# Mamba-and-experts kernel, second layer: decay loads and time steps placed earlier, and five products with C on VectorE in the last batch

## The chip, the core and the metric

The kernel runs on one core of one Trainium2 chip. The metric is the device time of one execution in microseconds. Five engines matter here: TensorE (PE in the profile, with PEld for its weight loads), VectorE (DVE), ScalarE (ACT), GpSimd (POOL) and SyncE (SP), which in this kernel issues nearly all DMAs. Every engine works through its own list of instructions in order, and the lists meet at semaphores.

## The reference

The model has two layers on 8 sequences ("batches") of 512 tokens with 128 features. Layer 0 is attention with a low-rank key and value path, plus a gated feed-forward part. Layer 1 adds a Mamba mixer and a mixture of experts to its input. Of layer 1 the change touches the mixer:

```python
h = _rmsnorm(x, norm_w); xz = h @ in_proj_w; u, z = split(xz)
u = silu(causal_depthwise_conv(u, conv_w, conv_b))
xdbl = u @ x_proj_w                      # dt_r (64), B (16), C (16)
dt = softplus(dt_r @ dt_proj_w + dt_proj_b)
def step(hst, inp):                      # over 512 time steps
    dA = exp(dt_t[..., None] * A)        # 256 channels x 16 states
    dBu = dt_t[..., None] * B_t[:, None, :] * u_t[..., None]
    hst = dA * hst + dBu
    y = einsum('bdn,bn->bd', hst, C_t)
y = (y + u * D) * silu(z);  return x + y @ out_proj_w
```

The experts are a shared gated block for every token and, of eight routed ones, the two best per token. Their rows are sorted into tiles of 256 rows, 24 tiles for each half of the batches; each tile is loaded with its expert's weights, computed and stored, and GpSimd later gathers the results back to the tokens.

## The kernel before

Layer 0 ends at about 483 us. From there the second layer goes through the 8 batches. In each, 256 channels times 16 states make 4096 recurrences, which are held as 32 **groups** of 128 partitions by 512 time steps; the loop variable `k` of every engine's `batch` function counts the groups, and each engine has its own `batch` (lines 1595, 1723, 1851, 1955 and 2102) in which the condition on `k` alone sets what is issued at which step. There is no scheduler: the order of the work on an engine is what these conditions write out. Batch `b` is in the loop while the inputs of batch `b + 1` are prepared (`nxt`) and the end of batch `b - 1` is finished (`old`).

One group goes like this. TensorE spreads dt times u over the states into one of two PSUM buffers (`spread_du`, L2029). VectorE multiplies it by B there (`inject`, L1922) and runs the recurrence with `tensor_tensor_scan` (`scan`, L1931) into one of 12 buffers `hs`. The scan's decays are exp(dt A): ScalarE computes them in place three groups ahead (`decay`, L1826) from dt rows that a DMA has repeated over the 16 states. GpSimd multiplies two groups at a time by C (`times_c`, L1681), and TensorE sums over the states, four groups at a time (`gather_y`, L2038). A scan whose buffer `hs` still holds a group that is not summed waits for `gathered`.

**The loads of decays** (`load_decays`, DMA at L1559) move 1 MB each, for four groups; I call the eight of a batch q0 to q7. There are four buffers for them at a time (their names in the profile are `decays`, `slots` and `y_xr`, since two of them live in memory that other data leave free), so the load for one quarter can start when the scans of the quarter four places before are done. SP waits for that (`scanned`) and for the dt rows to be in DRAM (`store_dt`, L1536).

**The time steps.** For batch `b + 1`: TensorE projects (`x_proj`, `dt_proj`), ScalarE and VectorE compute the softplus in parts (`dt_in`, `exp_z`, `one_more`, `log_in`, `softplus_cut` L1901, `softplus_end` L1906), GpSimd adds its parts and multiplies by u (`steps`, L1669 and L1673), SP stores dt to DRAM and then loads q0. In three bf16 parts dt times u goes to `block_in` through 24 small DMAs (`stack`, L1528), after ScalarE (`first_part`, `second_part`) and VectorE (`second_rest` L1911, `third_part` L1916) have split it.

**The experts** come along a table `plan` of due steps: SP loads rows (`load_rows`, L1499) and weights (`load_weights`, L1508) and stores results (`store_tile`, L1514), TensorE turns and multiplies (`turn_tile` L2048, `gate` L2064, `up`, `down`), ScalarE copies (`copy_xg` L1832, `copy_g` L1838, `weigh` L1845), VectorE and GpSimd do half each of the gated product (`half` L1944, `hidden` L1686). `fetch` (L1720) is the indirect DMA on GpSimd that brings results back; 20 of them stand in batch 8.

**The end of a batch** is `gather_y` of the last four groups, `skip` (L1937, adds u times D), `gate_y` (L1693, times silu z), `out_proj` (L2099) and `result` (L1952), then the store of the output (L1586).

## Time and profile before

| | us |
|---|---|
| median of 3 runs | 1230.9 (1224.32 to 1238.44) |
| the profiled execution, its own time | 1228.28 |
| its span, first to last instruction | 1226.5 |
| busy: DVE / PE / POOL / ACT | 938.6 / 871.2 / 701.0 / 505.5 |
| first scans of batches 1 to 8 | 483.1, 595.0, 689.1, 778.8, 870.1, 960.6, 1050.6, 1133.4 |

The profile is one execution. Its share of busy time is a mean over stages: in layer 0 and in layer 1 different engines are the limit, so the time of a batch of the second layer, from its first scan to the next batch's, is the number to read. Idle time stands in brackets behind the instruction that came after it, with what ended it.

### The profile page before, as it was taken

Reading aid. Unit: us, or ns where it says so; the run is one execution under the profiler, and the core shown is the slowest. Engines: PE = TensorE matmul, PEld = TensorE weight load, DVE = VectorE, ACT = ScalarE, POOL = GpSimd, SP = SyncE. Lnnn points to the kernel's source line nnn. Section 1 sums busy time; section 2 is a strip of 40 time slices with the busy share of each in tenths; the row PEclk is TensorE's granted clock in tenths of the full one; section 3 lists DMA queues with packets and bytes.
Section 4 is the critical chain, followed back from the end, with each engine's and each line's share of the span. In section 5 each row is a group of like instructions: output and inputs, shape, how many; then the busy total and the mean of one; then the engine's idle time right before and its main releaser. Section 6 shows DMA issues by size and latency. Waiting matters only on the chain. (4 is left out here: it accounts for less than half of the span.)

```text
span 1226.5 us, 12808 instructions
## 1 busy us (share of the span) xinstructions
PE 871.2 (71%) x3620; PEld 412.1 (34%) x3620; DVE 938.6 (77%) x1280; ACT 505.5 (41%) x840; POOL 701.0 (57%) x427
## 2 busy tenths in 40 slices
PE   3668988888888656676587687688777688664552
PEld 0123333333333323344244344344434344311120
DVE  3467787977977445799469879688979779899973
ACT  0112212123123322473376386385495485663230
POOL 1021122031113561379569877569989879789996
PEclk9568788788897867699689899797999889875575
DMA  4886746666450352767766766767877767646631
GB/s 127 208 180 144 187 140 153 184 171 152 118 142 14 99 155 63 155 145 165 185 196 176 188 207 167 158 215 172 207 217 169 182 207 174 206 141 126 163 86 28
DMA packets 102849, 192.30 MB, mean 157 GB/s; under 512 B 13147, under 2 KB 68124, under 8 KB 90364
## 3 DMA queue, kind: packets, MB, share of 16 engines
q1 hardware_dynamic: 91516, 183.07, 57.2%
q0 software_dynamic: 11264, 8.43, 4.2%
q8 instruction: 29, 0.48, 0.2%
q14 instruction: 40, 0.33, 0.1%
HBM read 146.80 MB, written 32.06 MB: 146 GB/s over the span
## 5 line engine op out<-in xcount | busy, mean ns | idle before, releaser
L1681 POOL TENSOR_TENSOR hs<-hs,c_rep 128x1024 f32<-128x1024 f32 x128 | 332.0, 2604 | 87.7 <-DVE hs L1931 86.9
L1922 DVE TENSOR_TENSOR p_s_du<-p_s_du,b_rep 128x512 f32<-128x512 f32 x256 | 175.4, 685 | 49.5 <-PE p_s_du L2029 46.2
L2029 PE MATMUL p_s_du<-block_in,spread 96*128 96x512 bf16 x256 | 112.9, 442 | 115.5 <-DVE hs L1931 109.0
L1931 DVE TENSOR_TENSOR_SCAN hs<-decays,p_s_du 128x512 f32<-128x512 f32 x132 | 161.1, 1221 | 13.5 <-DVE p_s_du L1922 0.5
L1931 DVE TENSOR_TENSOR_SCAN hs<-slots,p_s_du 128x512 f32<-128x512 f32 x100 | 122.1, 1221 | 19.7 <-ACT slots L1826 9.7
L802 DVE TENSOR_TENSOR value_prod<-p_eb_y_acc,v 128x512 f32<-128x512 f32 x128 | 83.9, 685 | 56.6 <-PE p_eb_y_acc L1109 47.1
L513 POOL TENSOR_TENSOR sc<-ex,ex_part 128x1024 f32<-128x1024 f32 x8 | 17.0, 2129 | 171.6 <-ACT ex_part L619 171.6
L1826 ACT ACTIVATE decays<-decays,a_neg 128x512 f32<-128x512 f32 x132 | 91.7, 718 | 49.4 <-DMA decays<-dt_rows 39.3
L1720 POOL DMA_INDIRECT y_xr<-moe_sums,position x64 | 105.4, 1647 | 10.8 <-issue 8.2
L1686 POOL TENSOR_TENSOR y_hid<-y_hid,g_in 128x512 f32<-128x512 f32 x64 | 99.0, 1548 | 20.3 <-DVE y_hid L1944 19.8
L2029 PEld LDWEIGHTS p_s_du<-block_in,spread 96*128 96x128 bf16 x256 | 26.1, 102 | 249.4 <-DVE hs L1931 179.0
L2038 PE MATMUL p_eb_y_acc<-hs,gather 128*32 128x512 f32 x512 | 84.3, 737 | 18.1 <-POOL hs L1681 18.1
L1826 ACT ACTIVATE slots<-slots,a_neg 128x512 f32<-128x512 f32 x100 | 68.6, 717 | 69.1 <-DMA slots<-dt_rows 69.0
L778 DVE TENSOR_TENSOR score_prod<-qb,p_k_misc 128x2048 f32<-128x2048 f32 x32 | 72.4, 2282 | 12.8 <-issue 7.4
L2064 PE MATMUL p_a_g<-xgt,wm 128*128 128x256 f32 x192 | 56.2, 419 | 25.6 <-ACT sg L1839 16.0
L1838 ACT ACTIVATE g_in<-p_a_g 128x512 f32<-128x512 f32 x64 | 38.1, 595 | 78.6 <-PE p_a_g L2064 46.7
L530 POOL TENSOR_TENSOR root<-var,half 128x8 f32<-128x8 f32 x8 | 13.2, 1648 | 96.3 <-DVE var L851 96.3
L2091 PE MATMUL p_acc_o<-wm,y_hid 128*128 128x128 f32 x384 | 60.9, 310 | 2.9 <-ACT os L1845 1.8
L2091 PEld LDWEIGHTS p_acc_o<-wm,y_hid 128*128 128x128 f32 x384 | 57.7, 223 | 10.2 <-POOL y_hid L1686 7.5
L2001 PE MATMUL p_k_misc<-y_ht,wtap 128*128 128x512 f32 x112 | 58.3, 618 | 0.0
L1073 PE MATMUL p_s_du<-score_prod,sum_d 128*32 128x512 f32 x256 | 46.8, 813 | 13.0 <-DVE score_prod L778 13.0
L2074 PE MATMUL p_a_u<-xgt,wm 128*128 128x256 f32 x192 | 54.5, 410 | 0.0
(193 smaller groups left out, 1751.6 us busy)
## 6 DMA issues: line engine op xcount, KB each, us to landing
decays<-dt_rows SPq DMA_DIRECT2D x33, 1024.0 KB
qb<-rq_rows SPq DMA_DIRECT2D x32, 1024.0 KB, 13.5
slots<-dt_rows SPq DMA_DIRECT2D x25, 1024.0 KB
wm<-in_wmoe SPq DMA_DIRECT2D x48, 384.0 KB
moe_rows<-zeros SPq DMA_DIRECT2D x8, 774.0 KB, 6.0
xg<-moe_rows SPq DMA_DIRECT2D x48, 129.0 KB
stack<-ex_part SPq DMA_DIRECT2D x96, 64.0 KB
block_in<-y_part SPq DMA_DIRECT2D x192, 32.0 KB
```

Source lines behind the costliest of these rows:

```text
L778: nc.vector.tensor_tensor(score_prod[:, i % 2], qb[:, i], p_k[:].unsqueeze(1).to_broadcast([128, 4, T]), ALU.mult)\
L802: nc.vector.tensor_tensor(value_prod[:, n % NP], p_eb[:, n % 2], v[:, b % NV], ALU.mult).then_inc(weighed.sem, 1)
L1681: nc.gpsimd.tensor_tensor(hs[:, n:n + 2], hs[:, n:n + 2], c_rep[p][:].unsqueeze(1).to_broadcast([128, 2, T]), ALU.mult)\
L1686: nc.gpsimd.tensor_tensor(hid[:, v % 2], hid[:, v % 2], g_in[:, v % 2], ALU.mult).then_inc(hid_done.sem, 1)
L1720: nc.gpsimd.indirect_dma_start(xr[:, b - 1, t], None, moe["sums"][grp], bass.IndirectOffsetOnAxis(ap=position[:, grp, kk, TT * i + t:TT * ...
L1826: nc.scalar.activation(decay_of, decay_of, ACT.Exp, scale=a_neg[:, g:g + 1]).then_inc(da_done.sem, 1)
L1922: nc.vector.tensor_tensor(p_du[:, k % 2], p_du[:, k % 2], b_rep[p][:], ALU.mult).then_inc(dbu_done.sem, 1)
L1931: nc.vector.tensor_tensor_scan(hs[:, n % NA], home(8 * (b - 1) + k // 4)[:, bass.ts(j, T)], p_du[:, k % 2], 0.0, ALU.mult, ALU.add).then_i ...
L2001: ins = nc.tensor.matmul(bank(b, U0 + n)[:, :], wtap[:, k, bass.ts(n, 128)], ht[:, b % 2, k:k + T], start=(k == 0), stop=(k == CONV - 1))
L2029: nc.tensor.matmul(p_du[:, k % 2], spread[:, i], block_in[:, (2 * b + s) % NB, j], start=True, stop=True).then_inc(du_full.sem, 1)
L2038: ins = nc.tensor.matmul(p_y[32 * j:32 * j + 32], w["gather"][:, i], hs[:, (GROUPS * (b - 1) + k) % NA], start=(i == 0), stop=(i == 3))
L2091: ins = nc.tensor.matmul(p_o[:, bass.ts(i, 128)], hid[:, v % 2, 256 * f + 128 * i:256 * f + 128 * i + 128], wm[:, j % NR, 2 * FF1 + 128 * ...
```

## The change

It touches the second layer alone, and every product, sum and load of before is still there. What it does:

- SP: the loads q3 to q7 of a batch move from steps 2, 6, 10, 14, 18 to 0, 4, 8, 12, 16; those of q0, q1, q2 of the next batch from 22, 26, 30 to 22, 24, 28. Within a step the decay load now comes first, then weights, then rows. Stores of expert tiles are issued two steps later, `repeat_bc` three later, `store_dt` and the first half of `stack` one sooner.
- The chain of time steps is one step sooner on TensorE and ScalarE, two on VectorE and GpSimd; on GpSimd `steps` and `hidden` now stand ahead of `times_c` in their step. The parts (`first_part` to `third_part`) are one step sooner.
- `gather_y` of the last quarter is one step sooner (2 for 3); `out_proj` and `result` are four steps later in all but the last batch (13 and 15 for 9 and 11).
- In batch 8 the products with C of pairs 3, 6, 9, 12 and 15 are done by VectorE right behind the scan of the pair's second group, in a new function; GpSimd does the other eleven. `gather_y` waits for both counts.

```diff
@@ -1319,6 +1319,7 @@
     QS = 30
     AHEAD = 3
     PAIRS = 5
+    BY_VECTOR = (3, 6, 9, 12, 15)
     SEG = GROUPS // ST
     TAPS = {14: (0, (0,)), 16: (0, (1,)), 17: (0, (2,)), 18: (0, (3,)), 20: (1, (0, 1)), 21: (1, (2,)), 22: (1, (3,))}
     shared, position, tile_expert, slots, second = w["shared"], moe["position"], moe["tile_expert"], moe["slots"], moe["second"]
@@ -1443,7 +1445,7 @@
                     plan.append((dict(rows=begin_at - 8 + 2 * h, weights=begin_at - 6 + 2 * h, turn=begin_at + h, gate=begin_at + 2 + h,
                                       hidden=then + 2 if h else begin_at + 6, up=then if h else begin_at + 4,
                                       half=then + 1 if h else begin_at + 5, down=then + 5 if h else then + 1,
-                                      weigh=then + 6 if h else then + 2, store=then + 8 if h else then + 4),
+                                      weigh=then + 6 if h else then + 2, store=then + 10 if h else then + 6),
                                  b, h, tile, len(plan) + 1))
     tile_unit = {tile: v for _, _, _, tile, v in plan if tile is not None}
 
@@ -1608,20 +1610,20 @@
                     tail(k)
                     if k == 23:
                         load_xr(0)
+                if b == 1 and k in (4, 8, 12, 15, 18):
+                    load_decays(1, {4: 3, 8: 4, 12: 5, 15: 6, 18: 7}[k])
+                if 1 < b <= B and k % 4 == 0 and k < 20:
+                    load_decays(b, (k + 12) // 4)
+                if nxt and k in (22, 24, 28):
+                    load_decays(b + 1, (k - 20) // 4)
+                for _, _, j, _ in due(b, k, "weights"):
+                    if j is not None:
+                        load_weights(j)
                 for _, _, j, _ in due(b, k, "rows"):
                     if j is not None:
                         load_rows(j)
-                for _, _, j, _ in due(b, k, "weights"):
-                    if j is not None:
-                        load_weights(j)
-                if b == 1 and k in (4, 8, 12, 15, 18):
-                    load_decays(1, {4: 3, 8: 4, 12: 5, 15: 6, 18: 7}[k])
-                if 1 < b <= B and k % 4 == 2 and k < 20:
-                    load_decays(b, (k + 10) // 4)
                 if b == 4 and k == 30:
                     load_xr(1)
-                if nxt and k % 4 == 2 and k > 20:
-                    load_decays(b + 1, (k - 22) // 4)
                 for _, _, j, _ in due(b, k, "store"):
                     if j is not None:
                         store_tile(j)
@@ -1633,12 +1635,12 @@
                 if nxt:
                     if k == 10:
                         store_bc(b + 1)
-                    if k == 16:
+                    if k == 19:
                         repeat_bc(b + 1, 1 - p)
-                    if k in (19, 21):
-                        store_dt(b + 1, (k - 19) // 2)
-                    if k in (21, 23, 24):
-                        stack(b + 1, 0, (21, 23, 24).index(k))
+                    if k in (18, 20):
+                        store_dt(b + 1, (k - 18) // 2)
+                    if k in (20, 22, 23):
+                        stack(b + 1, 0, (20, 22, 23).index(k))
                     if k in (25, 26, 27):
                         stack(b + 1, 1, k - 25)
                 if b == 7 and k in (1, 2, 3, 4):
@@ -1729,18 +1731,18 @@
                 turn = GROUPS * (b - 1) + k - 14
                 if 0 <= turn < 4 * GT and turn % 2 == 0:
                     send(*divmod(turn // 2, GT))
-                if old and k == 0:
-                    times_c(b - 1, q, GROUPS // 2 - 1)
-                if new and k and k % 2 == 0:
-                    times_c(b, p, k // 2 - 1)
+                if nxt and k in (16, 18):
+                    steps(b + 1, q, (k - 16) // 2)
                 for _, _, j, v in due(b, k, "hidden"):
                     hidden(v)
+                if old and k == 0 and b <= B:
+                    times_c(b - 1, q, GROUPS // 2 - 1)
+                if new and k and k % 2 == 0 and not (b == B and k // 2 - 1 in BY_VECTOR):
+                    times_c(b, p, k // 2 - 1)
                 if old and k == 5:
                     gate_y(b - 1, q, 1)
                 if new and k == 21:
                     gate_y(b, p, 0)
-                if nxt and k in (18, 20):
-                    steps(b + 1, q, (k - 18) // 2)
                 if (b, k) in bring:
                     fetch(*bring[b, k])
 
@@ -1872,20 +1874,19 @@
                 if k == 5:
                     silu_u(b + 1, q)
                     silu_z(b + 1, q)
-                if k == 9:
+                if k == 8:
                     copy_xd(b + 1)
-                if k in (11, 13):
-                    dt_in(b + 1, (k - 11) // 2)
+                if k in (10, 12):
+                    dt_in(b + 1, (k - 10) // 2)
+                if k == 12:
+                    exp_z(b + 1)
                 if k == 13:
-                    exp_z(b + 1)
-                if k == 14:
                     one_more(b + 1)
-                if k == 15:
                     log_in(b + 1)
-                if k in (20, 23):
-                    first_part(b + 1, (k - 20) // 3)
-                if k in (22, 25):
-                    second_part(b + 1, (k - 22) // 3)
+                if k in (19, 22):
+                    first_part(b + 1, (k - 19) // 3)
+                if k in (21, 24):
+                    second_part(b + 1, (k - 21) // 3)
 
         def main(tail):
             act.wait_ge(before["x1"].sem, before["x1"].at(B))
@@ -1931,6 +1932,12 @@
             nc.vector.tensor_tensor_scan(hs[:, n % NA], home(8 * (b - 1) + k // 4)[:, bass.ts(j, T)], p_du[:, k % 2],
                                          0.0, ALU.mult, ALU.add).then_inc(scanned.sem, 1)
 
+        def times_c(p, i):
+            dve.wait_ge(scanned.sem, scanned.at(B, 2 * i + 2))
+            n = (GROUPS * (B - 1) + 2 * i) % NA
+            nc.vector.tensor_tensor(hs[:, n:n + 2], hs[:, n:n + 2], c_rep[p][:].unsqueeze(1).to_broadcast([128, 2, T]), ALU.mult)\
+                .then_inc(hc_too.sem, 1)
+
         def skip(b, p, s):
             dve.wait_ge(gathered.sem, gathered.at(b, 4 * s + 4))
             dve.wait_ge(y_done.sem, y_done.at(b, s) if s else y_done.at(b - 1))
@@ -1958,26 +1965,28 @@
                 if new:
                     inject(b, p, k)
                     scan(b, k)
+                if b == B and k % 2 and k // 2 in BY_VECTOR:
+                    times_c(p, k // 2)
                 if tail:
                     tail(k)
                 for _, _, j, v in due(b, k, "half"):
                     half(v)
                 if old and k == 4:
                     skip(b - 1, q, 1)
-                if old and k == 11:
+                if old and k == (15 if nxt else 11):
                     result(b - 1)
                 if new and k == 20:
                     skip(b, p, 0)
                 if not nxt:
                     continue
-                if k == 16:
+                if k == 14:
                     softplus_cut(b + 1)
-                if k == 17:
+                if k == 15:
                     softplus_end(b + 1)
-                if k in (21, 24):
-                    second_rest(b + 1, (k - 21) // 3)
-                if k in (22, 26):
-                    third_part(b + 1, (k - 22) // 4)
+                if k in (20, 23):
+                    second_rest(b + 1, (k - 20) // 3)
+                if k in (21, 25):
+                    third_part(b + 1, (k - 21) // 4)
 
         def main(tail):
             schedule(batch, tail)
@@ -2030,7 +2039,12 @@
 
         def gather_y(b, q):
 
-            pe.wait_ge(hc_done.sem, hc_done.at(b, 2 * q + 2))
+            if b == B:
+                of_vector = sum(i < 2 * q + 2 for i in BY_VECTOR)
+                pe.wait_ge(hc_too.sem, hc_too.at(1, of_vector))
+                pe.wait_ge(hc_done.sem, hc_done.at(b, 2 * q + 2 - of_vector))
+            else:
+                pe.wait_ge(hc_done.sem, hc_done.at(b, 2 * q + 2))
             if q % 4 == 0:
                 pe.wait_ge(y1_done.sem, y1_done.at(b, q // 4) if q else y1_done.at(b - 1))
             for k in range(4 * q, 4 * q + 4):
@@ -2118,10 +2132,10 @@
                 for c, m, j, v in due(b, k, "down"):
                     down(v, c, m, j)
                 if nxt:
-                    if k == 8:
+                    if k == 7:
                         x_proj(b + 1, q)
-                    if k in (10, 12):
-                        dt_proj(b + 1, (k - 10) // 2)
+                    if k in (9, 11):
+                        dt_proj(b + 1, (k - 9) // 2)
                 if b + 2 <= B:
                     if k in TAPS:
                         project_u(b + 2, *TAPS[k])
@@ -2130,9 +2144,9 @@
                 if new:
                     if k >= 7 and k % 4 == 3:
                         gather_y(b, (k - 7) // 4)
-                if old and k == 3:
+                if old and k == 2:
                     gather_y(b - 1, GROUPS // 4 - 1)
-                if old and k == 9:
+                if old and k == (13 if nxt else 9):
                     out_proj(b - 1, 1)
                 if new and k == 24:
                     out_proj(b, 0)
```

Two places where the written order shows best. The first is SP's list near the end of batch 5, from the load of batch 6's q0 (its first row) over q1 to q2 (its last row); `slots` and `decays` are the buffers loaded. Before:

```order
411 L1559 DMA decays<-dt_rows 128x1x2048
412 L1514 DMA moe_sums<-os 128x2x128
...
416 L1508 DMA wm<-in_wmoe 128x768
417 L1489 DMA y_xt<-moe_xt 128x512
418 L1528 DMA block_in<-y_part 32x512 x12
419 L1499 DMA xg<-moe_rows 128x2x129
420 L1559 DMA slots<-dt_rows 128x1x2048
421 L1528 DMA block_in<-y_part 32x512 x8
422 L1499 DMA xg<-moe_rows 128x2x129
...
426 L1508 DMA wm<-in_wmoe 128x768
...
430 L1508 DMA wm<-in_wmoe 128x768
431 L1559 DMA slots<-dt_rows 128x1x2048
```

And of the changed kernel, the same three loads:

```order
426 L1561 DMA decays<-dt_rows 128x1x2048
427 L1530 DMA block_in<-y_part 32x512 x4
...
431 L1510 DMA wm<-in_wmoe 128x768
432 L1491 DMA y_xt<-moe_xt 128x512
433 L1530 DMA block_in<-y_part 32x512 x4
434 L1561 DMA slots<-dt_rows 128x1x2048
435 L1516 DMA moe_sums<-os 128x2x128
436 L1530 DMA block_in<-y_part 32x512 x4
437 L1501 DMA xg<-moe_rows 128x2x129
438 L1530 DMA block_in<-y_part 32x512 x8
439 L1561 DMA slots<-dt_rows 128x1x2048
...
443 L1510 DMA wm<-in_wmoe 128x768
```

Between q0 and q1 stood twelve `block_in` pieces and a load of rows, and now eight pieces and none; q2 now stands ahead of two loads of weights (`wm`). The second is the end of VectorE's list, of the changed kernel:

```order
1005 L1938 TENSOR_TENSOR hs<-hs,c_rep 128x1024
1006 L1923 TENSOR_TENSOR p_s_du<-p_s_du,b_rep 128x512
...
1015 L1932 SCALAR_TENSOR_TENSOR hs<-decays,p_s_du 128x512
1016 L1923 TENSOR_TENSOR p_s_du<-p_s_du,b_rep 128x512
1017 L1932 SCALAR_TENSOR_TENSOR hs<-decays,p_s_du 128x512
1018 L1938 TENSOR_TENSOR hs<-hs,c_rep 128x1024
1019 L1944 SCALAR_TENSOR_TENSOR y<-u,vecs,p_eb_y_acc 128x512
```

The product of the last pair (1018) now follows the last scan (1017) on the same engine; before, it was GpSimd's, at the end of its list.

## Rows read from the trace of the kernel before

**Rows 1.** Busy time of each engine, its share of the span, and instructions, from the page.

```profile
PE 871.2 (71%) x3620; PEld 412.1 (34%) x3620; DVE 938.6 (77%) x1280; ACT 505.5 (41%) x840; POOL 701.0 (57%) x427
```

**Rows 2.** One stretch per batch, 5 to 8, then the tail: busy per engine, clock, DMA.

```profile
core 0: us, PE busy (x) PEld busy (x) DVE busy (x) ACT busy (x) POOL busy (x), PEclk, DMA share, GB/s
870.10:960.60 90.50, 65.86 (x299) 36.77 (x298) 76.07 (x83) 55.14 (x99) 82.69 (x46) 0.93 0.77 197
960.60:1050.60 90.00, 70.26 (x315) 39.19 (x317) 75.57 (x84) 55.27 (x99) 78.73 (x44) 0.90 0.72 188
1050.60:1133.40 82.80, 48.70 (x181) 18.69 (x181) 78.08 (x77) 40.19 (x62) 67.85 (x38) 0.69 0.57 156
1133.40:1204.40 71.00, 36.21 (x131) 11.23 (x127) 60.91 (x68) 19.20 (x32) 67.55 (x38) 0.64 0.43 111
```

**Rows 3.** Waits from 590 us on: engine, line, waited for; us, times, longest.

```profile
DVE p_s_du L1922 <- PE p_s_du L2029: 42.7, 22, 10.4
DVE y L1937 <- PE p_eb_y_acc L2038: 24.5, 6, 12.7
DVE hs L1931 <- ACT y_xr L1826: 13.0, 4, 4.6
DVE hs L1931 <- ACT slots L1826: 9.7, 4, 4.6
...
ACT slots L1826 <- DMA slots<-dt_rows: 69.0, 11, 9.0
ACT decays L1826 <- DMA decays<-dt_rows: 30.4, 11, 5.0
ACT y_xr L1826 <- DMA y_xr<-dt_rows: 12.2, 3, 5.5
```

**Rows 4.** Timeline, start and duration: ScalarE, then VectorE, in batch 6.

```profile
967.95 0.72 ACT L1826 ACTIVATE slots<-slots,a_neg 128x512 f32<-128x512 f32 x1 [8.22 <-DMA slots<-dt_rows]
979.79 0.72 ACT L1826 ACTIVATE slots<-slots,a_neg 128x512 f32<-128x512 f32 x1 [4.97 <-DMA slots<-dt_rows]
986.20 1.95 ACT L1826 ACTIVATE slots<-slots,a_neg 128x512 f32<-128x512 f32 x3
986.96 1.22 DVE L1931 TENSOR_TENSOR_SCAN hs<-slots,p_s_du 128x512 f32<-128x512 f32 x1 [4.60 <-ACT slots L1826]
993.17 0.70 DVE L1922 TENSOR_TENSOR p_s_du<-p_s_du,b_rep 128x512 f32<-128x512 f32 x1 [2.48 <-PE p_s_du L2029]
```

**Rows 5.** Timeline of SP's queue between two decay loads: start, time to issue.

```profile
956.40 0.51 SPq L1499 DMA_DIRECT2D xg<-moe_rows  x1
957.96 1.55 SPq L1508 DMA_DIRECT2D wm<-in_wmoe  x2
959.72 0.68 SPq L1559 DMA_DIRECT2D slots<-dt_rows  x1
```

**Rows 6.** The chain that ended last, its end: start, us, what.

```profile
1157.43 1.15 issue
1158.58 1.55 POOL y_xr L1720
1160.13 2.37 POOL hs L1681
...
1212.64 2.37 POOL hs L1681
1215.01 2.85 issue
...
1219.20 2.09 PE p_eb_y_acc L2099 x8
```

**Rows 7.** Timeline of VectorE in batch 8 and at the end.

```profile
1169.16 0.70 DVE L1922 TENSOR_TENSOR p_s_du<-p_s_du,b_rep 128x512 f32<-128x512 f32 x1 [2.29 <-PE p_s_du L2029]
...
1188.69 0.70 DVE L1922 TENSOR_TENSOR p_s_du<-p_s_du,b_rep 128x512 f32<-128x512 f32 x1 [4.12 <-PE p_s_du L2029]
...
1202.39 0.68 DVE L1922 TENSOR_TENSOR p_s_du<-p_s_du,b_rep 128x512 f32<-128x512 f32 x1
1203.16 1.22 DVE L1931 TENSOR_TENSOR_SCAN hs<-decays,p_s_du 128x512 f32<-128x512 f32 x1
1217.06 0.75 DVE L1937 SCALAR_TENSOR_TENSOR y<-u,vecs,p_eb_y_acc 128x512 f32<-128x512 f32 x1 [12.68 <-PE p_eb_y_acc L2038]
```

**Rows 8.** Single lines: count, duration in ns (min, median, max), first and last start.

```profile
L1906 DVE TENSOR_TENSOR dtu<-conv,dtu x8: 1199/1200/1225, 422.8 to 1090.3; 128x1024 f32<-128x1024 f32 x8
L1911 DVE TENSOR_TENSOR conv<-dtu,y_part x16: 682/1867/3670, 438.5 to 1114.6; 128x512 f32<-128x512 f32 x16
L1916 DVE TENSOR_TENSOR y_part<-conv,y_part x16: 682/923/4586, 442.3 to 1122.0; 128x512 bf16<-128x512 f32 x16
```

**Rows 9.** TensorE's wait for weights, and a gate of batch 6, timeline.

```profile
590.45 2.07 PE L2064 MATMUL p_a_g<-xgt,wm 128*128 128x256 f32 x4 [9.57 <-DMA wm<-in_wmoe]
...
972.67 1.03 PE L2064 MATMUL p_a_g<-xgt,wm 128*128 128x256 f32 x4
```

More of the change, by code:

```diff
@@ L1403, in layer1 @@
     hc_done = count("hc_done", GROUPS // 2)
+    hc_too = count("hc_too", len(BY_VECTOR))
     gathered = count("gathered", GROUPS // 4)
@@ L1897, in vector @@
     def vector(dve):
-        start(dve, [sp_step, rest1, part3, dbu_done, scanned, y1_done, half_done, res_done])
+        start(dve, [sp_step, rest1, part3, dbu_done, scanned, hc_too, y1_done, half_done, res_done])
         def softplus_cut(b):
```

## The prediction

> **What bounds the kernel now.** I read the page's busy times first: VectorE works 77% of the span and no other engine is as near to full [rows 1]. A mean over stages says little, so next came a table with one stretch per batch. Batches 5 and 6 take 90.5 and 90.0 us with 76.1 and 75.6 us of VectorE's work; batch 7, which has only the shared expert's products left, takes 82.8 us with 78.1 us of work [rows 2]. So in a middle batch some 10 us go by in which VectorE has nothing to do, and without them a batch would take about 80.
>
> The waits say who is late. From 590 us on VectorE stood idle 42.7 us for TensorE's spread, 24.5 us for the sum over states before `skip`, and 13.0 + 9.7 us for ScalarE's decays, 89.9 us together [rows 3]. Of that 12.7 us lie behind the last scan [rows 7], 10.4 us are one wait at the start of batch 2 [rows 3], behind a gate that waited 9.57 us for weights [rows 9], and 2.29 + 4.12 us lie in batch 8 [rows 7]. That leaves 60.4 us for batches 2 to 7.
>
> Behind most of these stands one cause. ScalarE waited 69.0 + 30.4 + 12.2 us for loads of decays [rows 3]. Batch 6 shows how it reaches VectorE: ScalarE waits 8.22 us for q1 and 4.97 us for q2, does the copies and the silu of the next batch with their tables, and gets to the next decays at 986.20, so the scan starts 4.60 us late; TensorE stood in `x_proj` for the same silu, and the spread is 2.48 us late [rows 4]. An engine works in order, so a late load also holds ScalarE's copies for the experts, thereby TensorE's list, and thereby the sum that `skip` waits for.
>
> The last batch is another stage. The chain that ended last runs on GpSimd alone from 1158.58 to 1215.01: a product with C (2.37 us), a fetch, the next product [rows 6]. The last scan starts at 1203.16 and ends at 1204.4, and VectorE then waits 12.68 us [rows 7].
>
> **The loads of decays.** No work is removed; it is moved on queues. Before, q2 was issued at 959.72, behind a load of rows at 956.40 and two of weights at 957.96 [rows 5], and ScalarE had it at 979.79 [rows 4], 20.1 us later. Now it stands ahead of these: 959.72 - 956.40 = 3.3 us sooner at SP, and 2 x 384 + 129 KB less in front of it, which at the 188 GB/s of that batch [rows 2] is 4.8 us. The time steps come one step sooner, and a step is 90.0 / 32 = 2.8 us. Together 10.9 us against a wait of 4.97. q1 passes four `block_in` pieces and one load of rows: I put this at 3 us, an estimate from the 0.51 us of such an issue [rows 5] and as much for each piece, and with the step at 6 us against 8.22. Loads q3 to q7 come two steps sooner, and their waits were the small ones. So q2's wait should go, q1's fall to about 2 us, and what is late next is q0, at the head of a batch, which still stands behind `store_dt` and a `stack`.
>
> What speaks against taking all 60.4 us: the bytes are the same, and in 80 us instead of 90 their rate rises from 188 to 212 GB/s with DMA engines that were already busy 72 to 77% [rows 2]; weights and rows now stand behind 1 MB each; and SP stops at step 0, 4, 8 for scans, with everything behind it. The bounds are nothing and 60.4 us. I take 25 us, some 40%, which is 5 us in each of batches 2 to 6, nearer the lower end because each load that gains its place takes it from another. The wait at the start of batch 2 stays: q0 and a 1 MB load of x rows still precede its weights at the same steps.
>
> **The rest of the moves.** `repeat_bc` three steps later and stores of tiles two later only take waits from SP. `out_proj` and `result` four steps later cost nothing: the accumulator is next written by the shared expert's product at step 22, seven steps later; without that cover each step costs 2.8 us. The softplus one step sooner makes VectorE wait if ScalarE's logarithm is late: below 1 us a batch, and inside the 25. On GpSimd `steps` and `hidden` pass a product of 2.37 us, which TensorE needs for the sums; twelve buffers leave it four groups of room, so nothing.
>
> **The five products on VectorE.** GpSimd's chain starts behind `result` of batch 7, 1.3 us later than before, since the product of pair 3 now precedes it on VectorE. It then loses pairs 6, 9 and 12 ahead of pair 14, at 2.37 + 0.16 us each, 7.6 us, and pair 15 behind it, 4.1 us with the fetch between. The sum 1215.01 - 7.6 - 4.1 + 1.3 is 1204.6 us, when GpSimd is done with pair 14.
>
> VectorE's side: the nearest operation of this size with both inputs in SBUF took 1.200 us in the middle and 1.225 at most, in eight instances [rows 8]. With about 0.1 us for waiting on its own scan I count 1.3 us, 6.5 for five. The two waits in batch 8, 6.4 us, were TensorE behind GpSimd's lag and should go. So VectorE is done at 1204.4 - 6.4 + 6.5 = 1204.5 us at best: 10.5 us sooner than 1215.01.
>
> But other VectorE instructions beside GpSimd are stretched: L1911 took 0.682 us at least, 1.867 in the middle and 3.670 at most, L1916 0.682 to 4.586 [rows 8]. The Trainium skill, "SBUF — State Buffer", section "SBUF: two separate sides", has a rule that speaks against this change: a VectorE instruction with two SBUF inputs and a GpSimd instruction that reads SBUF exclude each other, and the second waits for the whole of the first. The trace bears it out in L1911 and L1916 and not in L1906, whose eight instances show no wait; by the rule in full the sum is that of the third rival.
>
> The price of one stretching is between 0 and 4.586 - 0.682 = 3.9 us; I take 1.2, the middle of L1911 less its minimum, for four of five, 4.5 us in all. That leaves **6 us** gained here, between 10.5 and a loss of 9. From the last product on the end is as before: sum, `skip`, `gate_y`, `out_proj` (2.09 us) [rows 6], `result`, store.
>
> **The sum.** The profiled execution took 1228.3 us by its own time (span 1226.5): 1228.3 - 25 - 6 = 1197.3 us. The median of the runs is 2.6 us above that execution, so against it I say **1200 us**, 2.5% less.
>
> **The rivals.**
> - *All of it comes back.* If q0's wait goes as well and the transfers keep up, 50 of the 60.4 us return: 1228.3 - 50 - 6 + 2.6 = 1175 us. For it: every wait named in rows 3 has the same root, and batch 7 runs at its work. Against it: batch 7 moved only 156 GB/s [rows 2]. Chance 0.18.
> - *The transfers are the limit.* A load of 1 MB took 20.1 us to be there; if that is the queue's own pace, an earlier issue means a longer way and only the tail is left: 1228.3 - 6 + 2.6 = 1225 us. For it: 77% busy in batch 5. Against: batch 5 moved 197 GB/s where batch 6 moved 188 [rows 2], so there was room. Chance 0.17.
> - *The stretching in full.* Each of the five products waits 3.9 us for GpSimd: 19.5 us, VectorE is done at 1204.5 + 19.5 = 1224 and the tail is 9 us longer, but the loads gain: 1228.3 - 25 + 9 + 2.6 = 1215 us. Against it: GpSimd spends only 2.37 us of some 4.1 in an arithmetic instruction. Chance 0.08.
> - *Slower: weights come late.* SP now stops for a scan and issues 1 MB before the weights of a batch's first tile. That gate ran at 972.67 [rows 9], 14.7 us after the issue at 957.96 [rows 5]. The new place costs 1 MB at 188 GB/s, 5.6 us, and so decides once the weights land more than 9 us after their issue. TensorE then stands with the spread behind the gate. Priced at 9.6 us, as once before [rows 9], in five batches: 48 us, and 1228.3 - 25 - 6 + 48 + 2.6 = 1248 us. Against it: the gates' own steps are unchanged, and only once did TensorE wait that long for weights [rows 9]. Chance 0.05.
>
> **How the numbers follow.** The forecast has what is left, 0.52, with a range of its own of 1186 to 1212, from 14 us more or 12 less of the 25. About 1% (12 us) is what a measurement of this kernel can tell from no change, so the line is at 1218.6. Under it are the forecast, the first rival, and most of the third: faster 0.78. Within 1% is mainly the second: 0.17. Slower is the fourth: 0.05. The range goes from 1177, which takes in about half of the first rival, to 1224, which takes in half of the second.
>
> **What would show it.** In the changed profile batches 2 to 6 should take about 85 us each; ScalarE's waits for decays, 111.6 us before, should be below 70, with q2's gone; the spread's 42.7 us should be near 25. In batch 8 the products on VectorE should take 1.2 us when undisturbed, up to 5 when not; `skip` should start 2 to 5 us behind the last of them. Wrong would be: batches still at 90 us with SP's loads sooner and landing no sooner (the second rival), TensorE waiting for `wm` in several batches (the fourth), or a last product later than 1215 - 25 = 1190 us.

## The result, and the profile after

The changed kernel is **slower**: 1272.0 us (median of 4 runs, 1267.86 to 1276.05) against 1232.9, ratio 1.032 (95% interval 1.025 to 1.040). Forecast were 1200 us. On another chip it came to 1.042 (1.034 to 1.051). Executions of one of these kernels on one chip scatter by up to 3.4%, and a ratio uses only those within 1.5% of the fastest of a kernel; where it matters I give the ratio of the medians of all runs beside it.

The profiled execution has a span of 1274.2 us, 47.7 more. First, the same stretches as in [rows 2], batches 5 to 8 (the last one here up to `skip`): length, busy time per engine, clock, share and rate of the DMA engines.

```profile
883.10:989.90 106.80, 73.60 (x316) 41.13 (x308) 82.15 (x84) 56.01 (x101) 80.69 (x47) 0.84 0.74 169
989.90:1098.50 108.60, 73.97 (x311) 40.07 (x306) 79.93 (x84) 56.31 (x101) 78.14 (x45) 0.81 0.71 154
1098.50:1183.10 84.60, 49.63 (x173) 18.22 (x172) 73.18 (x77) 41.97 (x65) 62.77 (x35) 0.66 0.59 160
1183.10:1264.80 81.70, 43.72 (x151) 12.28 (x151) 71.70 (x74) 17.29 (x28) 74.50 (x40) 0.60 0.47 97
```

Batches 5 and 6 are 16 and 19 us longer, while batch 7, without tiles of routed experts, is 1.8 us longer. VectorE's work grew by 4 to 6 us in 5 and 6, and the rest is idle. The rate of the transfers fell: the bytes are the same (192.30 MB on both pages), they took longer. The clock granted to TensorE fell too, from 0.93 and 0.90 [rows 2] to 0.84 and 0.81 in these two batches, and the same 2160 matmuls of the second layer kept it busy 527.3 us, before 509.0. How much of the loss comes of the slower clock no run separates.

The waits from 590 us on, as in [rows 3] (engine, line, waited for; us, times, longest):

```profile
DVE p_s_du L1923 <- PE p_s_du L2038: 94.7, 39, 9.6
DVE y L1944 <- PE p_eb_y_acc L2052: 2.6, 2, 2.1
DVE y_hid L1951 <- PE p_a_u L2088: 13.3, 6, 5.3
PE p_a_g L2062 <- DMA xg<-moe_rows: 61.3, 12, 9.4
PEld p_a_g L2062 <- DMA xg<-moe_rows: 65.7, 12, 9.7
ACT slots L1828 <- DMA slots<-dt_rows: 52.9, 9, 8.3
ACT decays L1828 <- DMA decays<-dt_rows: 32.2, 7, 6.7
SPq L154 <- DVE hs L1932: 144.7, 23, 12.4
```

What was forecast did happen in part: ScalarE's waits for decays fell from 111.6 to 85.1 us, VectorE's wait for ScalarE's decays is down from 22.7 to 0.5 us, and `skip`'s waits are nearly gone (24.5 to 2.6, of which 12.7 were the tail). In exchange TensorE stands 61.3 us in `turn_tile` for rows of expert tiles, and VectorE's wait for the spread behind it went from 42.7 to 94.7 us. SP stood for scans 144.7 us instead of 43.9. Of the kernel before, from 590 us on, the same waits:

```profile
PE p_a_g L2048 <- DMA xg<-moe_rows: 2.4, 1, 2.4
PEld p_a_g L2048 <- DMA xg<-moe_rows: 19.1, 7, 4.3
SPq L154 <- DVE hs L1931: 43.9, 11, 7.6
```

The second line is the one to read. A transposition on TensorE is a weight load (PEld) and a matmul (PE); the matmul's line is charged to whatever came last, here mostly ScalarE's copy of the tile before, while the weight load's line shows that the rows came hardly sooner. So the rows had next to no room already.

The whole account on VectorE, from the first scan to the end (743.4 and 796.3 us): its work grew by 24.6 us (610.6 to 635.2), its idle time by 28.3. Of the work 10.9 us are the five products and 11.5 us softplus and parts that took longer. In the idle time the 52.0 us more for the spread and 13.3 for the experts' `up` stand against 44 us less for `skip` and the decays.

The head of batch 6, SP's queue (start, time to issue), then TensorE and VectorE:

```profile
970.54 6.72 SPq L1530 DMA_DIRECT2D block_in<-y_part  x4
977.38 0.70 SPq L1501 DMA_DIRECT2D xg<-moe_rows  x1
978.20 12.19 SPq L1530 DMA_DIRECT2D block_in<-y_part  x8
990.57 0.65 SPq L1561 DMA_DIRECT2D slots<-dt_rows  x1
992.54 0.37 SPq L1510 DMA_DIRECT2D wm<-in_wmoe  x1
993.04 0.37 SPq L1501 DMA_DIRECT2D xg<-moe_rows  x1
```

The row of the weight load before the matmul, first in the kernel before, then in the changed one:

```profile
970.18 0.20 PEld L2048 LDWEIGHTS p_a_g<-ident,xg 128*128 128x128 f32 x2 [2.16 <-DMA xg<-moe_rows]
```

```profile
1013.70 0.29 PEld L2062 LDWEIGHTS p_a_g<-ident,xg 128*128 128x128 f32 x2 [9.22 <-DMA xg<-moe_rows]
```

```profile
1013.71 0.69 PE L2062 MATMUL p_a_g<-ident,xg 128*128 128x128 f32 x2 [8.72 <-DMA xg<-moe_rows]
```

```profile
1016.57 0.70 DVE L1923 TENSOR_TENSOR p_s_du<-p_s_du,b_rep 128x512 f32<-128x512 f32 x1 [8.89 <-PE p_s_du L2038]
```

Two things are to be seen. The rows issued at 993.04, behind q2, are used at 1013.70, 20.7 us later; before they were issued at 956.40 [rows 5], ahead of q2 and of the weights, and used at 970.18, 13.8 us later. They are thus 6.9 us longer on their way, and the wait for them is 7.1 us longer (9.22 for 2.16). They are also issued later, 3.2 us behind the batch's first scan where it was 4.2 us ahead of it. And q2 did not come sooner: it is issued 0.7 us *after* the batch's first scan at 989.9, and before 0.9 us ahead of it (959.72 and 960.6). The reason is in the `block_in` pieces: behind q1 stood eight, which took 6.20 us to be issued, and now twelve, which took 6.72 and 12.19 us. The same wait, of the second tile in batches 2 to 6, was 3.51, 2.86, 4.25, 2.74 and 2.16 us before and is 8.80, 7.13, 7.59, 9.73 and 9.22 now.

### The profile page after: what moved, and what is told of

Read it like the earlier page. It is cut to its first block and busy times, and to the rows that moved or that the text cites. A ratio compares the mean times of both kernels' runs of the same rounds, so it can differ in the third digit from the quotient of the medians.

```text
span 1274.2 us, 12815 instructions
## 1 busy us (share of the span) xinstructions
PE 872.5 (68%) x3620; PEld 407.8 (32%) x3620; DVE 963.0 (76%) x1285; ACT 506.4 (40%) x840; POOL 682.9 (54%) x422
## 2 busy tenths in 40 slices
DMA packets 102850, 192.30 MB, mean 151 GB/s; under 512 B 13148, under 2 KB 68125, under 8 KB 90365
## 5 line engine op out<-in xcount | busy, mean ns | idle before, releaser
L1683 POOL TENSOR_TENSOR hs<-hs,c_rep 128x1024 f32<-128x1024 f32 x123 | 313.2, 2547 | 69.6 <-DVE hs L1932 69.0
L1932 DVE TENSOR_TENSOR_SCAN hs<-decays,p_s_du 128x512 f32<-128x512 f32 x132 | 161.1, 1220 | 13.9 <-issue 0.5
L1688 POOL TENSOR_TENSOR y_hid<-y_hid,g_in 128x512 f32<-128x512 f32 x64 | 91.5, 1429 | 79.0 <-DVE y_hid L1951 78.7
L2052 PE MATMUL p_eb_y_acc<-hs,gather 128*32 128x512 f32 x512 | 93.6, 813 | 12.4 <-POOL hs L1683 9.4
L2078 PE MATMUL p_a_g<-xgt,wm 128*128 128x256 f32 x192 | 63.5, 463 | 27.5 <-ACT sg L1841 17.0
L2062 PE MATMUL p_a_g<-ident,xg 128*128 128x128 f32 x96 | 22.9, 327 | 63.3 <-DMA xg<-moe_rows 61.3
L1834 ACT ACTIVATE xgt<-p_a_g 128x256 f32<-128x256 f32 x48 | 18.3, 382 | 112.6 <-PE p_a_g L2062 110.9
```

The source lines that it names most:

```text
L1683: nc.gpsimd.tensor_tensor(hs[:, n:n + 2], hs[:, n:n + 2], c_rep[p][:].unsqueeze(1).to_broadcast([128, 2, T]), ALU.mult)\
L1688: nc.gpsimd.tensor_tensor(hid[:, v % 2], hid[:, v % 2], g_in[:, v % 2], ALU.mult).then_inc(hid_done.sem, 1)
L1932: nc.vector.tensor_tensor_scan(hs[:, n % NA], home(8 * (b - 1) + k // 4)[:, bass.ts(j, T)], p_du[:, k % 2], 0.0, ALU.mult, ALU.add).then_i ...
L2052: ins = nc.tensor.matmul(p_y[32 * j:32 * j + 32], w["gather"][:, i], hs[:, (GROUPS * (b - 1) + k) % NA], start=(i == 0), stop=(i == 3))
L2078: ins = nc.tensor.matmul(p_g[:, bass.ts(f, 256)], wm[:, j % NR, bass.ts(f, 128)], xgt[:, j % 2], start=True, stop=True)
```

## The experiments

In the diffs, "decays" stands for the lines with `load_decays`.

**e1_order_back, and again as j3.**

```diff
-decays (new steps); weights; rows
+rows; weights; decays (new steps)
```

> The changed kernel with one thing undone: within a step of SP's list, rows stand first, then weights, then the decay loads, as before; the new step numbers and all the rest stay. Theory A (rows and weights behind a 1 MB decay load come late, and TensorE stands in turn_tile for them, 61.3 us in the changed kernel): that wait falls below 20 us and the time to between 1205 and 1235 us. Theory B (SP stops for scans at steps 0, 4, 8 whatever stands ahead in the step, 144.7 us against 43.9, and what is behind it comes late): the time stays above 1255 us. Theory C (the chain of time steps, sooner, puts stretched VectorE instructions and GpSimd work in the way): above 1255 us too.

> The same kernel as e1 (the change with the order within a step undone everywhere), with more rounds, since its first interval was 0.9 to 3.7%. Theory A: 0.5 to 2% slower than before, the rest being the chain and the stops. Theory C (the chain is what remains): 1.5 to 2.5%.

Measured: 1.023 (1.009 to 1.037), then 1.012 (1.007 to 1.018); medians 1.011 and 1.017. Undoing the order alone returns some half to two thirds of the loss by j3 and by the medians (1.1 to 1.7% are left of 3.2 to 4.2), less by e1's ratio, whose interval is wide. Theory C isn't excluded by this pair: 1.7% lies in both expected ranges. The wait for rows fell to 14.5 and 15.8 us; one for weights of 36.6 and 35.1 us over the layer stands in its place.

**e3_queue_only, f2_steps_only, f3_order_only: the queue's part alone, and its halves.**

```diff
-rows; weights; decays at 2, 6, 10, 14, 18, 22, 26, 30
+decays at 0, 4, 8, 12, 16, 22, 24, 28; weights; rows      (e3)
+rows; weights; decays at 0, 4, 8, 12, 16, 22, 24, 28      (f2)
+decays at 2, 6, 10, 14, 18, 22, 26, 30; weights; rows     (f3)
```

> The kernel before with SP's loads as in the change (new steps, and decays, weights, rows in that order within a step) and nothing else. Theories A and B: it carries the loss, 1265 to 1285 us, with TensorE waiting for rows 40 us or more. Theory C: near 1233 us.

> The kernel before, with only the steps of the decay loads changed (0, 4, 8, 12, 16, 22, 24, 28); within a step rows and weights still stand first. Theory A (the place behind a 1 MB load within the step is what makes rows late): within 1% of before. Theory B (SP stops for scans at the new steps, and all that follows is late): at least 1.5% slower, SP's waits for scans above 130 us as in the changed kernel, and weights or rows late in several batches.

> The kernel before, with only the order within a step changed (decays, then weights, then rows); the decay loads keep their old steps 2, 6, 10, 14, 18, 22, 26, 30. Theory A: 1 to 3% slower, TensorE waiting for rows 15 us or more. Theory B: within 1% of before.

Measured: e3 1.034 (1.019 to 1.049; medians 1.022), f2 1.005 (1.001 to 1.009), f3 0.995 (0.990 to 1.000). The queue's part carries the loss, but neither half does. Both theories as I had put them miss: the two do harm only together. The wait for rows in e3 misses as well, 18.2 us where 40 or more were expected. In f2 and e3 (second line) the late ones are above all the `block_in` pieces, of which more now follow q1:

```profile
PE p_s_du L2029 <- DMA block_in<-y_part: 49.0, 7, 8.7
PE p_s_du L2029 <- DMA block_in<-y_part: 37.1, 6, 9.3
```

In the changed kernel this wait is 1.6 us: there the chain of time steps has the pieces ready sooner, and the rows are late instead. Which small load is late differs from version to version; in each a load of 1 MB has come to stand ahead of it. And f2 shows that a long wait on TensorE isn't yet a loss: with 49.0 us of it the time is 0.5% above.

**i1_stops_only: SP's stops without the loads.**

```diff
+if 1 < b <= B and k % 4 == 0 and k < 20: stop(b, (k + 12) // 4)
+if nxt and k in (22, 24, 28): stop(b + 1, (k - 20) // 4)
 rows; weights; decays (as before)
```

> The kernel before with SP's stops alone: at steps 0, 4, 8, 12, 16, 22, 24, 28, ahead of all else in the step, SP waits for the scans that a decay load there would wait for, and loads nothing; the loads stay where they were. Theory B: at least 1.5% slower, with SP's waits for scans at 130 us or more. Theory A: within 1% of before.

Measured: 0.993 (0.988 to 0.998; medians 0.998). The stops alone cost nothing. SP's waits for scans came to 102.7 us over the layer, not the 130 expected, so theory B falls only for stops of that length; longer ones follow in h1.

**h1_after_half, h2_before_half: half the bytes** in 48 of the 64 decay loads (the expectation says 25 of 32; the condition below takes 48, and the pages show 167.13 MB for 192.30).

```diff
-sp.dma_start(home(n), rows)
+these = slice(0, 2 * T if n >= 12 and not 30 <= n < 34 else 4 * T)
+sp.dma_start(home(n)[:, these], rows[:, :, these])
```

> The changed kernel with half the bytes in 25 of the 32 decay loads from the second batch's middle on: only the first two of four groups are moved, the other two use what the buffer holds. SP's stops, all steps and every order stay. Beside it h2 (the kernel before with the same halving). If rows and weights are late because 1 MB stands ahead of them in the queue (theory A), h1 comes within 1% of h2. If SP's stops for scans (theory B) or the chain (theory C) are what costs, h1 stays 2.5% or more above h2.

> The kernel before with half the bytes in the decay loads from the second batch's middle on, as in h1. All theories: ScalarE's waits for decays fall below 30 us from 111.6 and the time by 20 to 45 us, to 1185 to 1215 us.

Measured: 1193.8 us against 1178.8, 1.3% apart, where the full kernels are 3.2 to 4.2% apart. h2 is 3.2% below the kernel before (0.968, 0.959 to 0.977), 6 us lower than the range expected, and its waits for decays are 38.2 us, not below 30. Waits of h1, then of h2:

```profile
PE p_a_g L2063 <- DMA xg<-moe_rows: 16.4, 3, 9.6
SPq L154 <- DVE hs L1933: 194.7, 35, 12.4
```

```profile
ACT slots L1827 <- DMA slots<-dt_rows: 19.8, 4, 10.5
DVE p_s_du L1923 <- PE p_s_du L2030: 15.8, 12, 2.6
```

In h1 SP stops for scans even longer (194.7 us) and all steps are the change's, yet the wait for rows is a quarter. So it is the bytes, theory A, for about two thirds of the loss; the 1.3% that remain are just above the 1% that theory A allowed and well below the 2.5% of B and C. The halving lightens the queue and all transfers at once, so by itself it doesn't tell the place in the queue from the rate of all transfers; that the place matters is shown by j3, where the order alone was undone.

**f1_after_again, f4_rows_on_scalar.** f1 is the change, for comparison; f4 takes the rows out of SP's queue:

```diff
-sp.dma_start(xg[:, j % NX], ...)    # SP, step "rows"
+act.dma_start(xg[:, j % NX], ...)   # ScalarE, step "rows"
```

> The changed kernel once more, as it is, so that the parts below have it on their own chip. All theories: 3% slower than before, 2.5 to 4%.

> The changed kernel with the 48 loads of expert rows issued from ScalarE's queue instead of SP's, at the same steps; nothing else. If rows are late because they stand in SP's queue behind 1 MB decay loads and behind SP's stops (theories A and B alike), TensorE's wait for rows, 61.3 us in the changed kernel, falls below 15 us and the time by 15 us or more against the changed kernel. If it is the chain of time steps (theory C), or the rate of all transfers together, the time stays within 10 us of the changed kernel.

Measured: f1 1.042, f4 1.030 (1.023 to 1.038), 9 us less by the medians. The wait for rows is gone altogether, as expected; the time misses the 15 us of theories A and B and lies within the 10 us of the others. TensorE now stands in a tile's gate for its weights instead, which are still in SP's queue:

```profile
PE p_a_g L2081 <- DMA wm<-in_wmoe: 52.8, 8, 10.9
```

**j1_step28_back, j2_step0_back: where steps and order meet.**

```diff
+if k in (28,):  rows; weights     # j1; (0,) in j2
 decays; weights; rows (the others)
```

> The changed kernel with rows and weights ahead of the decay load at step 28 alone (q2 of the next batch); all other steps keep decays, weights, rows. Each part alone measured: new steps +0.5%, new order -0.5%, both +3.4%; with the table of due steps they differ from each other, from batch 2 on, only at steps 28 and 0. If the loss comes of the second row tile and the weights at step 28 standing behind q2, this returns most of what the whole order undone does: 1.0 to 1.5% faster than the changed kernel, 1.5 to 2.5% slower than before. If it is step 0, it stays 3 to 4% slower than before.

> The changed kernel with rows and weights ahead of the decay load at step 0 alone (q3). If the loss comes of step 28: 3 to 4% slower than before, as the changed kernel. If it comes of step 0: 1.5 to 2.5% slower than before.

Measured: j1 1.043 (1.038 to 1.048), j2 1.025 (1.016 to 1.034; medians 1.034), and j3, both and more, 1.012 on the same chip. TensorE's waits of j1, then of j2:

```profile
PE p_a_g L2086 <- DMA wm<-in_wmoe: 52.3, 10, 8.6
PE p_a_g L2070 <- DMA xg<-moe_rows: 18.4, 8, 4.6
```

```profile
PE p_a_g L2070 <- DMA xg<-moe_rows: 60.6, 10, 11.1
PE p_a_g L2086 <- DMA wm<-in_wmoe: 8.9, 2, 4.9
```

My expectation for step 28 was wrong. With it undone TensorE waits less for the rows (18.4 us), and the weights of step 30, behind q2, are awaited instead. A tile needs both. For step 0 the runs don't decide: j2's ratio says a part comes back, its medians (3.4%) say none.

**e4_chain_only, again as l2; g1_no_chain; l1_order_and_chain_back: the chain of time steps.**

```diff
-x_proj 8, dt_proj 10/12, softplus 16/17, steps 18/20, ...
+x_proj 7, dt_proj 9/11, softplus 14/15, steps 16/18, ...     (e4, l2)
 the change, without that edit                                 (g1)
 the change, without that edit and with rows; weights; decays  (l1)
```

> The kernel before with only the chain of time steps sooner (TensorE, ScalarE, VectorE, GpSimd, stores of dt, first half of the stacks, repeat_bc three later, GpSimd's steps and hidden ahead of times_c). Theories A and B: 1215 to 1238 us, a little faster if q0 comes sooner. Theory C: 1255 us or more, with softplus_cut stretched from 1.2 to about 2.9 us a batch.

> The same kernel as e4 (before, with the chain of time steps sooner alone), with more rounds, since its interval was -0.3 to 2.6%. If the chain costs by stretched VectorE instructions (7 to 10 us more of them in the traces): 0.5 to 1.2% slower. If it costs nothing by itself: within 0.4%.

> The changed kernel without the chain of time steps sooner (SP's loads, their order, stores later, out_proj and result later, products on VectorE as in the change). If the two parts simply add, this has what the queue alone had (3.4%, interval 1.9 to 4.9) less the tail: 2 to 3% slower than before. If the chain is what makes the queue's part worse (the changed kernel 3.2 to 4.2%), it is 1.5 to 2.5% faster than the changed kernel.

> The changed kernel with the order within a step undone and the chain of time steps undone; left are the new steps of the decay loads, stores two later, out_proj and result later, and the products on VectorE. With the chain in it (j3) it was 1.2% slower than before (0.7 to 1.8). If the chain is what remained: within 0.5% of before, by new steps +0.5% and tail -0.5%. If the new steps, stores and out_proj are what remained: 1 to 1.5% slower.

Measured: e4 1.011 (0.997 to 1.026), l2 1.017 (1.004 to 1.029), so the chain alone costs something between nothing and 1.7% (medians 1.001 and 1.008). g1 is 1.029 (1.021 to 1.037), 0.3 to 1.3% below the changed kernel. There TensorE waits 39.6 us for `block_in` and 29.0 for rows, so both are late, as in e3. l1 is 1.022 (1.008 to 1.037; medians 1.011), where j3, with the chain in, is 1.012 (medians 1.017): the two can't be told apart, and l1 and l2 both rest on two executions of the kernel before. VectorE's `softplus_cut`, in the changed kernel and, as the chain's own doing, in e4 (second line):

```profile
L1902 DVE SCALAR_TENSOR_TENSOR dtu<-conv,dtu x8: 1212/2892/4035, 417.2 to 1132.6; 128x1024 f32<-128x1024 f32 x8
```

```profile
L1900 DVE SCALAR_TENSOR_TENSOR dtu<-conv,dtu 128x1024 f32<-128x1024 f32 x6 | 17.6, 2934 | 0.0
```

It took 1.33 us in the mean of the same six batches before. From L1901, L1906, L1911 and L1916 together VectorE has 10 us more from batch 2 on in the changed kernel (63.6 to 73.6) and 7 us more in e4. The trace shows why for `softplus_cut`. Batch 3's of the changed kernel, GpSimd first, and then the same two of the kernel before:

```profile
732.10 2.34 POOL L1683 TENSOR_TENSOR hs<-hs,c_rep 128x1024 f32<-128x1024 f32 x1
732.64 2.89 DVE L1902 SCALAR_TENSOR_TENSOR dtu<-conv,dtu 128x1024 f32<-128x1024 f32 x1
```

```profile
733.83 2.33 POOL L1686 TENSOR_TENSOR y_hid<-y_hid,g_in 128x512 f32<-128x512 f32 x1
733.85 1.20 DVE L1901 SCALAR_TENSOR_TENSOR dtu<-conv,dtu 128x1024 f32<-128x1024 f32 x1
```

Now it starts while GpSimd's product runs and ends 1.09 us behind it, about its own undisturbed length. Before it started as the product ended, and GpSimd's next instruction was the long one (2.33 us, where the median of its line is 1.28).

**e2_tail_only, g4_tail_order.** e2 has the five products on VectorE alone, g4 these and f3's order.

```diff
+BY_VECTOR = (3, 6, 9, 12, 15)     # e2
+decays; weights; rows             # g4: at the old steps
```

> The kernel before with the five products of the last batch on VectorE and nothing else. All theories leave this part alone. From the last batch of the changed kernel (first scan to skip 77.3 us against 83.7) it should be 6 us faster, 1226 us, 0.5%; if the products were stretched to 3.9 us each it would be 9 us slower.

> The kernel before with the two parts that alone measured a little below it: the products of the last batch on VectorE (ratio 0.9985, interval 0.992 to 1.005) and the order decays, weights, rows at the old steps (0.9951, 0.9903 to 0.9999). If the two add: 0.5 to 1% faster than before. If they are noise: within 0.5%.

Measured: e2 0.9985 (0.992 to 1.005; medians 0.989), g4 **0.987** (0.980 to 0.994; medians 0.995). g4 has the lowest ratio of the versions that move all bytes, but by the medians it is within 0.5%, which was the range expected of noise; f3 and i1 lie below 1 by their intervals too. (The 77.3 us that the expectation of e2 gives for the last batch of the changed kernel are misread; the trace has 81.7, from 1183.1 to `skip` at 1264.8, against 83.6. The profiled execution of e2 has 83.7, that of g4 76.1.) The tail of g4:

```profile
1189.08 1.22 DVE L1933 TENSOR_TENSOR_SCAN hs<-decays,p_s_du 128x512 f32<-128x512 f32 x1
1190.33 1.23 DVE L1939 TENSOR_TENSOR hs<-hs,c_rep 128x1024 f32<-128x1024 f32 x1
1193.62 0.75 DVE L1945 SCALAR_TENSOR_TENSOR y<-u,vecs,p_eb_y_acc 128x512 f32<-128x512 f32 x1 [2.06 <-PE p_eb_y_acc L2053]
```

From the last scan to `skip` it is 4.5 us, where it was 13.9 [rows 7].

## Why the prediction was wrong

**What bounds the kernel** was read rightly: ScalarE's waits for decays stand behind VectorE's idle time, and h2 agrees, where halving their bytes takes 37 us off by the medians and ScalarE's waits for them fall from 111.6 to 38.2 us. It isn't the only cause, though: TensorE's turns stood for rows as well, 2.16 to 4.25 us in each of batches 2 to 6, and fewer bytes of decays bring these sooner too. And what h2 shows is a statement about bytes in a queue, where I took it for one about issue times.

**The step that failed is "the loads of decays"**, with its 25 us gained. I let q2 pass two loads of weights and one of rows and counted what q2 gains, 3.3 + 4.8 us, and nothing for the three that it passed. They lose what it gains: the rows took 13.8 us from issue to use and now take 20.7. And they had no room: the rows of step 28 were issued at 956.40 and turned at 970.18, and the weight load of that turn stood 2.16 us for them already. The prediction named the danger ("weights and rows now stand behind 1 MB each") and put no price on it in the sum. I looked at TensorE's matmul line for `xg`, which has 2.4 us before, and took it for room; the weight load's line, 19.1 us in seven waits, says the opposite. The table of dues needed one more line: for each load that is passed, its issue, its first use, and how long the queue took in between.

q2 itself wasn't sooner, since the same reasoning holds for the `block_in` pieces behind q1 (twelve, 18.9 us to issue, for eight in 6.2). So the 10.9 us that the sum gives q2 were not there at all: relative to the first scan it was issued 1.6 us later.

**The rivals.** The one that came true is the fourth, "weights come late", at 0.05, with 1248 us. Its place was off by one operand (rows first, and weights as soon as the rows are in time, f4 and j1), and its decision point was reckoned for the weights alone. That its price, 48 us, is near the 52.0 us that VectorE waited more for the spread is luck: other waits fell by 44 us, and 24.6 us of the longer time are VectorE's own work. The 25 us on the other side of that sum did not come. "The transfers are the limit" was right as a mechanism but has no side on which nothing is lost: an issue order on a full queue is a choice of who is late. That is argued from the waits of e3, f2, f4 and j1; g4 and f3 show that not every order loses.

**The rest of the moves.** "Below 1 us a batch" for the softplus was too little: its stretched instruction cost 1.6 us a batch (1.33 to 2.88), for the same reason that I priced for the products on VectorE and not here. I had looked at L1906, which is never stretched, and not at its neighbour of the same size, which was so in the kernel before:

```profile
L1901 DVE SCALAR_TENSOR_TENSOR dtu<-conv,dtu x8: 1198/1202/2723, 421.5 to 1086.5; 128x1024 f32<-128x1024 f32 x8
```

Alone the chain costs at most some 1% by the medians.

**The products on VectorE.** Of 6 us, e2 shows between 10 gained and 6 lost by its interval. The mechanism held: the last product took 1.22 us, `skip` came 2.1 us behind it, and the five took 1224 ns at least and 5450 at most:

```profile
L1938 DVE TENSOR_TENSOR hs<-hs,c_rep x5: 1224/1225/5450, 1203.3 to 1261.5; 128x1024 f32<-128x1024 f32 x5
```

One of five was stretched, by 4.2 us, and a second by less; the price of 4.5 us for all was about right. From batch 8's first scan to `skip` the changed kernel is 1.9 us shorter, less than the 6, in a single trace. The last product starts at 1261.51, so the sign of being wrong that the prediction gave for it (later than 1190) came true as well.

**What stays open.** After the order is undone 1.2% remain (j3), and about as much in h1 over h2. The chain alone may cost that, yet taking it out as well (l1) isn't shown to lower the time; there TensorE waits 37.2 us for `block_in`. So without the chain sooner those pieces are late, with it VectorE's instructions are stretched; that this explains the whole rest is argued, not shown. The slower clock of TensorE and the four steps that `out_proj` and `result` were moved were not taken apart either. Why i1 measured slightly below the kernel before is not known.

## What to carry to other kernels

On a queue as full as this one, where 129 KB took 14 to 21 us from issue to use, putting one load sooner makes what it passes later. Before moving it, list for each passed load its issue and its first use. Where an instruction waits for several things, a wait list names the last of them; the one that came just before it has no slack either, and here the line of the weight load shows it. To learn whether a place or a volume is the trouble, take two runs: undo the order and leave the bytes, and halve the bytes and leave the order.

## What the runs showed of the hardware

- 129 KB of rows, issued behind 1 MB and 384 KB, took 20.7 us to their use, and 13.8 us in the kernel before, where they stood ahead of both. The issue of eight 32 KB pieces took SP 12.19 us in such a stretch and 6.20 in the kernel before: the crowded queue shows on the issuing engine too.
- Half the bytes in 48 of the 64 decay loads gave 3.2% (h2), more than any order of the same bytes that was tried.
- The 48 loads of rows issued from ScalarE (f4) were never awaited, while SP's own weights were, for 52.8 us.
- A VectorE instruction of 128x1024 with two inputs in SBUF took 1.20 us undisturbed and 2.89 us when it started 0.54 us into GpSimd's product of 2.34 us; when it started first, GpSimd's instruction was the long one, 2.33 us for a median of 1.28.
